# Moving the query projection of all heads into the feed-forward phase of a fused attention and feed-forward block

## What is computed

```python
q = (x @ Wq + bq).reshape(b, h, t, dh)                          # 16 heads, dh = 128
k = (x @ Wk + bk).reshape(b, t, h, dh).transpose(0, 2, 3, 1)
v = (x @ Wv + bv).reshape(b, t, h, dh).transpose(0, 2, 1, 3)
logits = einsum('bhtd,bhds->bhts', q, k) * scale                # causal mask, softmax
out = einsum('bhts,bhsd->bhtd', weights, v) ... @ Wo + bo
ffn = (silu(xn @ w_gate.T) * (xn @ w_up.T)) @ w_down.T          # hidden 1024
```

## Time and profile before

| | us |
|---|---|
| median of three runs | 2147.22 |
| the three runs | 2148.16, 2147.22, 2143.95 |
| the profiled execution, its time | 2148.62 |
| the profiled execution, its span from first to last instruction | 2146.8 |
| busy in the span: PE, PEld | 2114.7, 1942.7 |
| busy in the span: DVE, ACT, POOL | 1383.4, 1150.2, 975.9 |
| HBM traffic | 47.34 MB read, 16.78 MB written |

### The profile page before, as it was taken

How to read it: one execution, slowest core, us unless ns; L and a number is a source line. 1 busy time by engine, 2 the same in 40 slices (tenths; PEclk the granted TensorE clock), 3 DMA queues, 4 the chain that set the end, 5 groups by cost and what they waited for, 6 DMA issues and landing times.

```text
span 2146.8 us, 37887 instructions
## 1 busy us (share of the span) xinstructions
PE 2114.7 (99%) x13937; PEld 1942.7 (90%) x13937; DVE 1383.4 (64%) x3038; ACT 1150.2 (54%) x2536; POOL 975.9 (45%) x1200
## 2 busy tenths in 40 slices
PE   8999999999999999999999999999999999999998
PEld 6788898999999999999999999999999999999997
DVE  7323217575767767676767575757676676767675
ACT  4111126556565655656565655565656556565654
POOL 4545464344544444444444343445444444444442
PEclk9999999999999999999999999999999999999999
DMA  6111130000000111000001010000001110000000
GB/s 218 50 40 49 40 104 15 16 16 16 16 9 16 55 40 30 16 16 16 16 11 60 6 57 16 16 16 16 10 15 55 40 31 16 16 16 16 9 6 20
DMA packets 60679, 66.56 MB, mean 31 GB/s; under 512 B 3488, under 2 KB 54864, under 8 KB 59216
## 3 DMA queue, kind: packets, MB, share of 16 engines
q1 hardware_dynamic: 60496, 64.13, 9.3%
HBM read 47.34 MB, written 16.78 MB: 30 GB/s over the span
## 4 chain that ended last, share of the span: by engine, by line
PE 94%; DVE 3%; issue 1%; ACT 1%; POOL 1%; DMA 0%; DVEq 0%; POOLq 0%; ACTq 0%
PE s_ps L885 37%; PE m_ps L885 23%; PE o_ps L1052 19%; PE t_ps L1034 12%; PE o_ps L885 2%; DVE xn_sb L759 1%; ACT qT L679 1%; DVE stats L732 0%; PE t_ps L911 0%; DVE sil L797 0%; DMA x_sb<-in_L_attn_x 0%; POOL x_sb L547 0%; POOL hid_lo L536 0%; POOL q_lo L536 0%; DVE mean_var L735 0%
## 5 line engine op out<-in xcount | busy, mean ns | idle before, releaser
L597 POOL TENSOR_SCALAR prob<-prob,inv_sum 128x128 f32<-128x128 f32 (+7 forms) x512 | 384.4, 751 | 973.4 <-DVE inv_sum L859 973.4
L850 DVE TENSOR_REDUCE neg_max<-s_ps 128x1 f32<-128x128 f32 (+7 forms) x512 | 388.1, 758 | 17.4
L692 ACT ACTIVATE prob<-s_ps,neg_max 128x128 f32<-128x128 f32 (+7 forms) x512 | 382.3, 747 | 11.7 <-DVE neg_max L850 11.7
L875 DVE TENSOR_TENSOR pT_diag_lo<-t_ps,pT_diag_hi 128x128 fp32r<-128x128 f32 (+3 forms) x512 | 247.7, 484 | 196.8 <-ACT pT_diag_hi L714 196.7
L1034 PE MATMUL t_ps<-ident,prob 128*128 128x128 f32 x2304 | 339.3, 274 | 5.3 <-DVE pT_full_lo L875 3.0
L714 ACT ACTIVATE pT_diag_hi<-t_ps 128x128 fp32r<-128x128 f32 (+3 forms) x512 | 225.1, 440 | 178.1 <-PE t_ps L1034 178.1
L885 PE MATMUL s_ps<-k_hi,q_hi 128*128 128x384 f32 (+5 forms) x768 | 302.1, 393 | 0.8 <-ACT prob L692 0.8
L1034 PEld LDWEIGHTS t_ps<-ident,prob 128*128 128x128 f32 x2304 | 267.5, 140 | 34.8 <-POOL prob L597 7.1
L885 PE MATMUL s_ps<-k_hi,q_lo 128*128 128x384 f32 (+5 forms) x768 | 263.2, 343 | 0.0
L885 PE MATMUL s_ps<-k_lo,q_hi 128*128 128x384 f32 (+5 forms) x768 | 262.2, 341 | 0.0
L875 DVE TENSOR_TENSOR pT_full_lo<-t_ps,pT_full_hi 128x512 fp32r<-128x512 f32 x256 | 174.3, 681 | 73.4 <-ACT pT_full_hi L714 73.3
(11 more groups left out here) (178 smaller groups left out, 5692.2 us busy)
## 6 DMA issues: line engine op xcount, KB each, us to landing
wk_raw<-in_L_attn_Wk SPq DMA_DIRECT2D x64, 128.0 KB, 2.7
wv_raw<-in_L_attn_Wv SPq DMA_DIRECT2D x32, 256.0 KB, 2.8
wo_raw<-in_L_attn_Wo SPq DMA_DIRECT2D x32, 256.0 KB, 2.8
x_sb<-in_L_attn_x SPq DMA_DIRECT2D x8, 512.0 KB, 9.4
xnT_dram<-xnT_a_hi SPq DMA_DIRECT2D x8, 512.0 KB, 3.1
xnT_dram<-xnT_a_lo SPq DMA_DIRECT2D x8, 512.0 KB, 3.9
base_dram<-y_stage SPq DMA_DIRECT2D x16, 256.0 KB, 2.1
xnT_hi<-xnT_dram SPq DMA_DIRECT2D x4, 1024.0 KB, 4.8
```

Of the source, the lines that this page charges most:

```text
L597: eng.tensor_scalar(prob[:, j % 3, 0:L], prob[:, j % 3, 0:L], inv_sum[:, j % 4:j % 4 + 1], 1.0, ALU.mult, ALU.mult).then_inc(s_norm, 1)
L692: eng.activation(prob[:, j % 3, 0:L], s_ps[j % 2][:, c0:c1], ACT.Exp, bias=neg_max[:, j % 4:j % 4 + 1], accum_out=row_sum[:, j % 4:j % 4 + ...
L850: eng.tensor_reduce(neg_max[:, g % 4:g % 4 + 1], s_ps[g % 2][:, c0:c1], AX_X, ALU.max, negate=True).then_inc(s_max, 1)
L875: eng.tensor_tensor(lo, t_ps_used(tb, i, bank), hi, ALU.subtract).then_inc(s_tlo, 1)
```

## The change

The Q pieces leave the attention phase. Their work is done in the feed-forward phase: after the eight `gate_up` of chunk c, `project_q(c)` multiplies all 16 column blocks of Wq (128 columns each) with the chunk's 512 tokens, straight from `xnT_a`. One such block is 6 matmuls of 512 moving columns, and lands in `t_ps[cb % 2]`. ACT adds the bias and writes it to `q_stage` (two slots, each for two blocks), in the space of the raw weights, and SP stores a full slot to `q_dram` (512 KB, in runs of 128 elements or 512 bytes). `down(c)` follows `project_q(c)` at once, so `hid` needs one buffer only. Wq is loaded earlier, after the second "up" transposes, and is split in chunk 0 after `ht` 6 by ACT and DVE, with the scale folded in. In the attention phase SP loads the query of each head, 512 KB, into `q_raw`, and `split_q` reads it with a step of 64 elements. K, V and y pieces get new places. The first K and V pieces follow `down(7)` directly.

```diff
-K_AT = [((0, E), (1, E)), ((2, E), (3, E)), ((0, E), (1, E)), ((0, L), (6, E))]
-V_AT = [((6, E),), ((1, E), (6, E), (7, E)), ((4, L), (5, L), (6, E)), ((7, E),)]
-V_AT_BATCH_END = ((5, E), (5, L), (7, E), (8, L))
-Q_AT = ((1, E), (1, L), (2, E), (2, L), (3, E), (3, L), (4, E), (4, L))
+K_AT = [((0, E), (1, E)), ((1, E), (2, E))]
+V_AT = ((3, E), (4, L), (6, E), (7, E))
...
-    before = [("Q", 0, m) for m in range(8)] + [("K", 0, 0), ("K", 0, 1)] + [("V", 0, m) for m in range(4)]
+    before = [("K", 0, 0), ("K", 0, 1)] + [("V", 0, m) for m in range(4)]
...
     for n in range(NHD - 1):
...
+        put("K", n + 1, n * NI, K_AT[n % 2])
+        if n % 2:
+            put("V", n // 2 + 1, n * NI, V_AT)
...
-        hid = sb2("hid", [P, 2, HT, CH], a)
+        hid = sb2("hid", [P, HT, CH], a)
+        wq = sb2("wq", [P, KT, HD], a)
...
+        q_stage = raw_w[:, 0:2 * 2 * CH].rearrange("p (b h c r) -> p b h c r", b=2, h=QH, c=2)
...
-        qT = sb("qT", [P, GROUP, T], F32)
+        q_raw = sb("q_raw", [P, 2, RQ, QTOK], F32)
...
+        BIAS_AT, WQ_AT = 5, 6
+        def q_ps(cb):
+            return t_ps[cb % 2][:, :]
...
@@ SP
+            for j, src in enumerate((bq, bk, bv)):      # before w_down, was after the last x
+                eng.dma_start(bias_rows[j * NH:(j + 1) * NH, :], src.rearrange("(h p) -> h p", p=P)).then_inc(s_bias, 16)
...
+            def store_q(c):
+                for c2 in range(RQ // 2):
+                    u = c * RQ // 2 + c2
+                    eng.wait_ge(s_qout, 2 * u + 2)
+                    dst = q_dram[QH * c:QH * (c + 1), :, 2 * c2:2 * c2 + 2, :]
+                    eng.dma_start(dst.rearrange("h p c r -> p h c r"), q_stage[:, u % 2]).then_inc(s_qst[u % 2], 16)
...
             store_xnT(0)
+            eng.wait_ge(s_ta, a_bank_no[("wu", KT - 1, 1)] + 1)
+            eng.dma_start(wq_raw, Wq_rows).then_inc(s_wqraw, 16)
             for c in range(NC):
                 if c + 1 < NC:
                     store_xnT(c + 1)
...
+                store_q(c)
+                store_base(c)
...
+            def load_q(n):
+                if n >= 2:
+                    eng.wait_ge(s_q, 2 * (n - 1))
+                eng.dma_start(q_raw[:, n % 2], q_dram[n]).then_inc(s_qload[n % 2], 16)
...
+                if n + 2 < NHD:                          # last in the SP queue of head n
+                    load_q(n + 2)
...
@@ POOL
-                        if c >= 2:
-                            eng.wait_ge(s_down, 2 * (c - 1))
+                        if c:
+                            eng.wait_ge(s_down, 2 * c)
...
             def split_q(n, half):
-                if n % GROUP == 0 and half == 0:
-                    eng.wait_ge(s_qout, out_count[("Q", n // GROUP, 7)])
+                if half == 0:
+                    eng.wait_ge(s_qload[n % 2], 16 * (n // 2 + 1))
                 if n:
                     eng.wait_ge(s_qk, NI * (n - 1) + 4 * (half + 1))
-                split(q, qT[:, n % GROUP, half * BANK:(half + 1) * BANK], s_qhi, s_q, lambda t: t[:, half, :])
+                rows = slice(half * QTOK // 2, (half + 1) * QTOK // 2)
+                split(q, q_raw[:, n % 2, :, rows].rearrange("p c r -> p r c"), s_qhi, s_q,
+                      lambda t: t[:, half, :].rearrange("p (r c) -> p r c", c=RQ))
...
@@ ACT
+            def wq_hi():
+                eng.wait_ge(s_wqraw, 16)
+                for kt in range(KT):
+                    eng.activation(wq[0][:, kt, :], wq_raw[:, kt, :], ACT.Copy, scale=SCALE).then_inc(s_wqhi, 1)
+
+            def q_hi(c):
...
+                for cb in range(RQ):
+                    j = c * RQ + cb
+                    u = j // 2
+                    eng.wait_ge(s_qfill, j + 1)
+                    if u >= 2 and cb % 2 == 0:
+                        eng.wait_ge(s_qst[u % 2], 16 * (u // 2))
+                    eng.activation(q_stage[:, u % 2, :, cb % 2, :], q_ps(cb).rearrange("p (h r) -> p h r", h=QH),
+                                   ACT.Identity, bias=bqs_sb[:, cb:cb + 1]).then_inc(s_qout, 1)
...
@@ DVE
+            def wq_lo():
+                for kt in range(KT):
+                    eng.wait_ge(s_wqhi, kt + 1)
+                    eng.scalar_tensor_tensor(out=wq[1][:, kt, :], in0=wq_raw[:, kt, :], scalar=SCALE,
+                                             in1=wq[0][:, kt, :], op0=ALU.mult, op1=ALU.subtract).then_inc(s_wq, 1)
...
@@ PE
+            def project_q(c):
+                if c == 0:
+                    eng.wait_ge(s_wq, KT)
...
+                for cb in range(RQ):
+                    j = c * RQ + cb
+                    if j >= 2:
+                        eng.wait_ge(s_qout, j - 1)
+                    terms = [(parts(wq, lambda t: t[:, kt, cb * P:(cb + 1) * P]),
+                              parts(xnT_a, lambda t: t[:, c % 2, kt, :])) for kt in range(KT)]
+                    product(q_ps(cb), terms).then_inc(s_qfill, 1)
...
-                if c >= 1:
-                    down(c - 1)
-            down(NC - 1)
+                project_q(c)
+                if c == 0:
+                    eng.wait_ge(s_bcol, 1)
+                down(c)
```

More of the change, by code:

```diff
@@ L114, in plan_pieces, with put @@
 def plan_pieces():
-    before = [("Q", 0, m) for m in range(8)] + [("K", 0, 0), ("K", 0, 1)] + [("V", 0, m) for m in range(4)]
+    before = [("K", 0, 0), ("K", 0, 1)] + [("V", 0, m) for m in range(4)]
     early = {g: [] for g in range(LAST + 1)}
     late = {g: [] for g in range(LAST + 1)}
-    def put(what, j, start, places, first=0):
-        for m, (i, where) in enumerate(places, first):
+    def put(what, j, start, places):
+        for m, (i, where) in enumerate(places):
             (early, late)[where][start + i].append((what, j, m))
@@ L130, in plan_pieces @@
     for n in range(NHD - 1):
[L131 to L138, removed]
+        put("K", n + 1, n * NI, K_AT[n % 2])
+        if n % 2:
+            put("V", n // 2 + 1, n * NI, V_AT)
     order, bank = list(before), {}
     for j, piece in enumerate(before):
-        bank[piece] = ("m", 0, 1)[j % 3]
+        bank[piece] = (0, 1, "m")[j % 3]
     for g in range(LAST + 1):
@@ L169, in attention_ffn_block @@
     piece_no = {piece: j for j, piece in enumerate(pieces)}
[L172 to L176, removed]
+    out_count, before_in_bank, latest = {}, {}, {}
+    for j, piece in enumerate(pieces):
+        out_count[piece] = j + 1
         before_in_bank[piece] = latest.get(bank_of[piece])
@@ L487, in store_out @@
                 eng.dma_start(out_rows[:, t0:t0 + 2, :], y[:, 2 * j:2 * j + 2, :]).then_inc(s_out[j], 16)
+            def load_q(n):
+                if n >= 2:
+                    eng.wait_ge(s_q, 2 * (n - 1))
+                eng.dma_start(q_raw[:, n % 2], q_dram[n]).then_inc(s_qload[n % 2], 16)
+            eng.wait_ge(s_up, NC * HT)
+            for slot in range(2):
+                eng.wait_ge(s_xst[slot], 32 * (NC // 2))
+            load_xnT(0)
             load_wk(0)
             load_wv(0)
+            store_q(NC - 1)
+            eng.wait_ge(s_qout, QB)
+            for slot in range(2):
+                eng.wait_ge(s_qst[slot], 4 * QB)
+            load_q(0)
+            load_q(1)
             load_wk(1)
+            store_base(NC - 1)
             load_wo(0)
@@ L640, in _ @@
                         part_hi(b)
-            eng.wait_ge(s_biasT, 1)
-            eng.activation(bias[:, :], t_ps[0][:, 0:3 * NH], ACT.Copy).then_inc(s_bcol, 1)
-            eng.wait_ge(s_bcol, 1)
-            eng.activation(bqs_sb[:, :], bq_sb, ACT.Copy, scale=SCALE).then_inc(s_bqs, 1)
-            eng.wait_ge(s_bqs, 1)
-            eng.wait_ge(s_ffn, 2 * NC)
+                    if c == 0 and ht == BIAS_AT:
+                        bias_columns()
+                    if c == 0 and ht == WQ_AT:
+                        wq_hi()
+                q_hi(c)
             eng.wait_ge(s_hid, NC * HT)
-            for slot in range(2):
-                eng.wait_ge(s_yst[slot], 16 * NC)
             def piece_out(piece):
@@ L666, in piece_out @@
                     if j == 0 and m == 0:
-                        eng.wait_ge(s_wq, 4)
+                        for slot in range(2):
+                            eng.wait_ge(s_yst[slot], 16 * NC)
                     if j >= 2:
@@ L804, in _ @@
                         part_lo(b)
-                if c >= 1:
-                    base_out(c - 1)
-            base_out(NC - 1)
+                    if c == 0 and ht == WQ_AT:
+                        wq_lo()
+                base_out(c)
             eng.wait_ge(s_bcol, 1)
@@ L985, in issue_piece @@
                     ins = product(ps, terms)
-                elif what == "V":
+                else:
                     if m == 0:
```

104 lines of the change are left out of this document (40 added, 64 removed).

## The result

The changed kernel takes 2150.92 us (median of 15 runs, 2148.55 to 2156.0); the kernel before, beside it, takes 2147.02 us (15 runs, 2143.95 to 2148.88). The ratio is 1.0022, with a 95% interval of 1.0015 to 1.003. It is slower by 0.2%, which the interval just tells from no difference. Forecast were 2135.5 us and a range up to 2150: the time lies just above the range, and the sign is wrong.

The account below looks back on a forecast made before the run. PE's instruction order was taken to bound the kernel nearly everywhere. PE work -18.7, start +2 and attention +5 gave -11.7 us from 2148.6, so 2136.9, as a median 2135.5 us; range 2127 to 2150, forecast band 2128 to 2142.

Parts of the forecast that it names:

- PE's work: Q products on PE: 193.0 us removed from attention, 174.3 us added in eight chunks, net 18.7 us less.
- between the phases: Passage from feed-forward to attention: K and V work covers ACT's wait for the y_stage stores, nothing lost.
- The strided read of POOL: split_q in attention: reading with a step of 64 elements costs 0 to 8 us in all, 1 taken.
- I take 3.5, hidden: Query stores in project_q: each lands in 3.5 us, under the 4.0 us limit, so PE does not wait.
- the upper bound: Query stores in project_q: at 4.6 us landing, 48 slots wait 0.28 us each, 13 us in all.
- 5 forecast: Attention phase: costs 5 us more than its PE work, from POOL's read, batch starts, head 0 and small waits.
- For small waits elsewhere I add 2 us: Attention phase: an allowance of 2 us for small waits not named one by one.
- 1 us for the three: Three batch starts in attention: the query load ahead of the K weights delays their split, 1 us in all.
- 1 for head 0: First head of attention: less filler without V in step 6, 1 us.
- +2 forecast: Start of feed-forward: 5.4 us off, 7.4 added by the Wq split wait and lower clock, net plus 2 us.
- (1): Rival: stores pace project_q; 2148 us at 4.6 us a store, 2158 at 5 us; chance 0.13.
- (2): Rival: in attention, POOL's strided reads or DVE's backlog delay norms and take PE's place; 2142 to 2164 us; chance 0.17.

Follow-up runs that it names:

- plain read: Changed kernel with split_q reading q_raw with unit step, which permutes the query rows: 2151.77 us, ratio 1.0019 to the kernel before.
- the four losses repaired: Changed kernel with four store slots, K weights ahead at batch starts, DVE's start order and one V piece moved from step 4: 2124.81 us, ratio 0.9895.
- later load: Changed kernel with the 2 MB activation load put behind the last chunk's query stores in SP's queue: 2145.59 us, ratio 0.9989.
- VectorE's new order: Changed kernel with the Wq split one step earlier and later row tiles' statistics behind chunk 0: 2146.75 us, ratio 0.9996.
- V pieces in other places: Changed kernel with one V piece moved from the odd head's step 3 to the even head's step 6: 2157.91 us, ratio 1.0045.
- the V piece moved alone: Changed kernel with one V piece moved from the odd head's step 4 to the even head's step 6, step 3 kept: 2143.5 us, ratio 0.9989.
- the three edits: Changed kernel with four store slots, K weights ahead at batch starts and DVE's new order at the start: 2132.19 us, ratio 0.9925.

## Why the prediction was wrong

**Right.** PE's work: 21.76 us a chunk against 21.79. Nothing is lost between the phases. The stores' median, 3.2 us (3.5 taken). The strided read of POOL: dearer by 0.78 us a half and hidden, as the plain read showed.

**The step that failed** is "I take 3.5, hidden". It puts one landing time in for 64 stores and compares that with the limit. The path does not wait for the median. The limit itself was 3.7 us and not 4.0, so with 3.2 typical it waits for each store that is more than 0.5 us late and whose slot is wanted again in the same chunk. Four such cost 10.7 us, near the 13 of the upper bound, but by another way; that nearness is luck. The largest was to be seen in the order of the change: its SP queue has the 2 MB load of the activations ahead of `store_q(7)`, and I had followed SP's queue only in the attention phase. And what I had written for the start, that such an idle time is followed by the lower clock, holds here too and makes 4.3 us into 7.1. The other three could not be read from the trace of before; a bound for a late store could have been set.

**Mis-sized in attention:** 5 forecast, 8.7 measured. The term "For small waits elsewhere I add 2 us" is 6.5 (31 pairs, 0.21 us each), from one wait of 0.26 us in step 6 of the even head. I had noted that even heads lose the V piece of this step, "on PE and on DVE alike", and took that for neutral. It was not: the piece had covered the low part of DVE, and put back there (with step 3 left alone) it gave the 0.23 us a pair back. The batch starts, "1 us for the three", are 4.4. The mechanism was right (the query load ahead of the K weights), and only the size was off. The size also differs between executions: where only the stores' slots were changed, the same three starts lose 6.3 us. The rest, head 0 and the last head, is 2.2 us under the due time, where I had put 1 for head 0.

**Mis-sized at the start, the other way:** +2 forecast, 0 measured. The wait (4.2 lost, 4.4 forecast) came as described, the lower clock behind it costs 1.7 instead of 3, and what the change takes off elsewhere in the start is 5.9 instead of 5.4.

**The rivals.** (1) was written as all stores at 4.6 us; what came was a few slow ones. Its 13 us were near the 10.7, but the place and the way are not its own. (2) was right in kind, not in the engine: POOL's strided reads cost nothing, DVE's low part 0.21 us a pair. That is 0.11 us a head, half of the 0.23 from which the rival alone turned the sign; it took the stores as well. With the four losses repaired, the kernel takes 2124.81 us, 1% under the kernel before; the start's repair in it concerns a loss that the kernel before has in its own way.

**Left open.** Why single stores of 0.5 MB land late in chunks 0, 2, 3, 5 and 6. It happens at nearly the same places in the kernels with four slots and with the later load, with the instruction packet beside it, and no run here varied that packet. Also open are the spread between executions of one kernel, 5 to 7 us, and the last head, which takes between 43.3 and 45.4 us in the profiled executions.

## What to carry to other kernels

Where a buffer's turn leaves less than a microsecond over a transfer's median, price the late transfer, not the median, allow for the lower clock that followed most of the waits of 2 us and more here, and read the whole queue ahead of the transfer; two more slots in space that lies free cost nothing. Filler pieces between dependent steps are cover: when one is removed, name what it covered, and when one is moved, look at the place that it leaves too. A change that takes 19 us off the bounding engine can be eaten by four losses of 4 to 11 us in different places, each cheap to repair once it is seen.

## What the hardware showed

- A store of 512 KB in 512-byte runs lands in 3.2 us (median of 64 in the changed kernel), but seven take 4.4 to 8.0. The five of them without a load ahead (4.4 to 5.1) run at full rate and then with a tail of 7 to 25 GB/s; the other two (8.0 and 6.8) left behind the loads for attention.
- PE's idle times of 4.0 and 4.1 us were followed by stretches of the lower clock that cost 1.7 and 2.8 us more; behind one of 1.4 us (VectorE's new order) and the smaller gaps at the stores the clock stayed at 1.00. In between both happened: at the batch starts, waits of 1.92 us (changed kernel), 1.99 (plain read) and 2.09 (four slots) were followed by 1.00, but waits of 1.86 (plain read) and 1.90 (later load) by 0.62 and 0.57, and those of 2.33 to 3.36 (V pieces in other places) by 0.50 to 0.56. So the length of a wait does not by itself tell here whether the clock falls.
- POOL's pass over 512 columns with a step of 64 elements takes 1.13 us where the plain one takes 0.62; with a second, plain operand 1.56 against 1.29.
- Executions of the kernel before lie at 2143.7 to 2145.3 us where the mean granted clock is 0.999 and at 2146.8 to 2149.5 where it is 0.995 or 0.996 (27 runs, beside the V piece moved alone, the later load, the start and the three edits; four of them, at 2145.8 to 2146.3, have 0.998), so part of the spread goes with the clock.
